# Squares in their own buffer, a fourth PSUM bank in turn, the solve on one engine, one convolution tap and the update keys on ScalarE and GpSimd, and an order table per chunk

## The reference, cut to what matters

```
xn = layernorm(x)
qkv = silu(causal_conv4(xn @ W_qkv.T))            # 2048 channels, 4 taps for each
z = xn @ W_z.T;  beta = sigmoid(xn @ W_b.T);  g = -exp(A_log) * softplus(xn @ W_a.T + dt_bias)
q, k = l2norm per head (8 heads of 64, each used by 2 of the 16 value heads);  v: 16 heads of 64
for t:  S = S * exp(g_t);  d = (v_t - k_t S) * beta_t;  S += k_t (x) d;  o_t = q_t S
x = x + (norm_weight * rmsnorm(o) * silu(z)) @ W_out.T
h = rmsnorm(layernorm(x)) * norm_w;  scores = softmax(h @ router_w.T), 32 experts, the top 4 of each token
x = x + layernorm(x) + sum over 4 of w_e * (silu(h w1_e) * (h u_e)) w2_e + shared expert(h)
```

## Time and profile before

| what | value |
|---|---|
| median of 3 runs | 1326.2 us (1325.64 to 1330.1) |
| profiled execution, its own time | 1323.6 us |
| its span | 1321.7 us |
| busy PE / DVE / POOL / ACT | 989.4 / 823.2 / 618.0 / 455.4 us |
| mean granted clock of TensorE | 0.832 |
| DMA, mean over the span | 125 GB/s |

### The profile page before, as it was taken

One profiled execution on the slowest core, in us unless ns is written; L12 is line 12 of the kernel. 1 busy time (PEld: TensorE's weight loads), 2 busy tenths in 40 slices (PEclk: granted clock), 3 DMA queues, 4 the chain that ended last, 5 costly groups with the idle time before them and its releaser, 6 DMA issues.

```text
span 1321.7 us, 32155 instructions
## 1 busy us (share of the span) xinstructions
PE 989.4 (75%) x12359; PEld 810.8 (61%) x12359; DVE 823.2 (62%) x1947; ACT 455.4 (34%) x890; POOL 618.0 (47%) x907
## 2 busy tenths in 40 slices
PE   0673687787688879868787986878685799998950
PEld 0662675676577667657666765766675457776730
DVE  5169469569848956984895698489544243333335
ACT  1331422542253244225324422532422124444420
POOL 2036248447545744764484476448343013554530
PEclk9776789698778969877896987789588699999985
DMA  5270232505253360535336152533685922444437
GB/s 206 83 190 18 70 85 52 163 22 153 71 152 104 103 173 23 153 66 157 103 98 173 29 153 66 157 97 83 185 282 186 358 69 81 126 134 123 118 124 222
DMA packets 182356, 165.61 MB, mean 125 GB/s; under 512 B 75699, under 2 KB 174908, under 8 KB 181312
## 3 DMA queue, kind: packets, MB, share of 16 engines
q1 hardware_dynamic: 172272, 144.60, 38.9%
q0 software_dynamic: 7632, 16.87, 4.0%
q10 hardware_dynamic: 2304, 2.10, 0.5%
HBM read 66.03 MB, written 101.55 MB: 127 GB/s over the span
## 4 chain that ended last, share of the span: by engine, by line
PE 44%; DVE 34%; issue 9%; DMA 6%; ACT 4%; SPq 1%; POOL 1%; DVEq 0%; POOLq 0%; ACTq 0%
DVE arena L785 9%; PE ps L1039 5%; PE ps L1187 5%; PE ps L1249 5%; DVE arena L427 5%; DVE arena L424 4%; PE ps L1171 3%; PE ps L1102 3%; PE ps L1048 2%; PE ps L1092 2%; PE ps L1111 2%; PE ps L1272 2%; DMA out<-work 2%; PE ps L1156 2%; DMA work<-htd 2%
## 5 line engine op out<-in xcount | busy, mean ns | idle before, releaser
L785 DVE SCALAR_TENSOR_TENSOR arena<-ps,cw,arena 128x256 f32<-128x256 f32 x384 | 156.1, 475 | 84.2 <-ACT arena L600 83.1
L1039 PE MATMUL ps<-work,arena 128*128 128x259 f32 x512 | 162.6, 454 | 26.9 <-DVE arena L785 24.6
L557 POOL DMA_INDIRECT picked<-work x95 | 93.4, 983 | 111.4 <-DVE work L974 66.1
L1039 PEld LDWEIGHTS ps<-work,arena 128*128 128x128 f32 x512 | 107.4, 222 | 55.7 <-DVE arena L785 29.4
L600 ACT ACTIVATE arena<-ps,cw 128x256 f32<-128x256 f32 x128 | 60.2, 470 | 198.9 <-PE ps L1039 198.4
L546 POOL DMA_INDIRECT slotted<-hr,slots x64 | 63.3, 989 | 138.7 <-DVE slots L931 124.0
L964 DVE TENSOR_TENSOR work<-work,ps 128x128 f32<-128x128 f32 (+1 forms) x111 | 34.0, 307 | 140.6 <-ACT work L700 116.1
L477 POOL TENSOR_TENSOR rn<-rin,mhalf 128x16 f32<-128x16 f32 x16 | 46.5, 2906 | 153.7 <-DVE rin L791 153.7
L1249 PE MATMUL ps<-arena,work 128*128 x380 | 100.7, 387 | 7.4 <-issue 6.2
L427 POOL TENSOR_TENSOR arena<-arena 128x60 f32<-128x60 f32 (+29 forms) x248 | 92.1, 372 | 19.4
L424 POOL TENSOR_TENSOR arena<-arena 128x60 f32<-128x60 f32 (+29 forms) x248 | 89.4, 360 | 24.1 <-DVE arena L827 7.8
(11 more groups left out here) (221 smaller groups left out, 2234.7 us busy)
## 6 DMA issues: line engine op xcount, KB each, us to landing
slotted<-blank SPq DMA_DIRECT2D x17, 4128.0 KB
arena<-in_w SPq DMA_DIRECT2D x2, 6528.0 KB, 20.1
work<-slotted SPq DMA_DIRECT2D x95, 129.0 KB
arena<-tab SPq DMA_DIRECT2D x64, 128.0 KB, 3.5
work<-tab SPq DMA_DIRECT2D x64, 128.0 KB
arena<-picked SPq DMA_DIRECT2D x16, 512.0 KB, 4.6
work<-xtd SPq DMA_DIRECT2D x8, 259.0 KB, 3.4
arena<-in_x SPq DMA_DIRECT2D x1, 2048.0 KB, 8.4
```

What stands on the lines that cost most here:

```text
L557: g.indirect_dma_start(out=picked, out_offset=bass.IndirectOffsetOnAxis(ap=to, axis=0), in_=yrow[:, j % SLOTS, :], in_offset=None, bounds_ ...
L785: v.scalar_tensor_tensor(out=acc_, in0=bank_of("proj", p, s_, i)[:, k:k + W2], scalar=cw[:, u, k:k + 1], in1=acc_, op0=ALU.mult, op1=ALU.a ...
L1039: ins = mm(to[:, 0:WX], wqkv[:, k, m:m + P], xt2[:, p % 3, k, :], start=k == 0, stop=k == KD - 1)
```

## The change

It has seven parts.

1. The squares get a buffer of their own, `sq` (`carve(KT, W2)`), four rows instead of eight, so `silu` no longer waits for the solve of the pair before; it waits for `ss_mm` of the two groups before. `at` holds 6 chunks instead of 8.
2. Tap 1 moves from DVE to ACT: `mul` writes taps 0 and 1 into two places, DVE's `tap` does taps 2 and 3 (four instructions), and a new item `sum` on POOL adds the two places before `silu`.
3. The solve's elimination runs on DVE alone, all columns. A new ACT item `lg` (three copies) puts `ntx` in order, so that `lx` is one transpose of 128 partitions.
4. `up` goes. A new POOL item `ktb` multiplies the keys by the negative beta and decay for the chunk, `ku` multiplies them with the copied u (`us`) and waits for `ue` and `ktb`; it has 16 products of 64x64 instead of 8 of 64x128.
5. KU shares the bank of UR, and the bank so freed is the fourth one in turn. `z`, `ht`, `rt` and `rank` take banks in turn too; `yt` and `op` keep W3.
6. `tc` is split in `ta` (the copies that need only the transposes) and `tc`; `ht` on ACT in `hr` and `htb`.
7. The table is new, with `PAIR = 95.20`, a time for each step of the solve, and for each of a pair's four chunks and two blocks a row of its own. It starts a pair's convolution while the pair before is being solved.

The diff, cut to its core:

```diff
-PAIR, CHUNK = 84.0, 21.0
-FRONT = [(20, "blank"), (60, "xload"), (62, "dload"), (10.5, "ss", 0), (16.9, "kt", 0), (17, "kt", 1), (13, "ssq", 0), (13.2, "rpow", 0),
+TURNS = 4
+PAIR = 95.20
+FRONT = [(-89.34, "nd", 0), (-88.1, "nd", 1), (-60.93, "proj", 0, 0), (-59.88, "proj", 0, 1), (-59.83, "xload"), (-59.78, "blank"),
...
-        return [("tap", 6 * (8 * p + ix[0]) + 5 + ix[1])]
+        return [("tap", 4 * (8 * p + ix[0]) + 3 + ix[1])]
+    if name == "z":
+        return [("zs_out", 4 * p + ix[0] + 1)]
...
+        ktb = carve(KR, DH)
+        sq = carve(KT, W2)
-        W = banks[0:3]
-        W3, KS, QS, UR, KU = banks[3:8]
-        O, U = (KS, QS), (UR, KU)
+        W = banks[0:TURNS]
+        W3, KS, QS, UR = banks[TURNS:8]
+        KU = UR
+        O, U = (KS, QS), (UR, W[3])
...
+                if name == "sum":
+                    p, s_ = ix
+                    f = 8 * p + s_
+                    pool.wait_ge(S["tap"], 4 * f + 4)
+                    pool.wait_ge(S["mul_out"], 4 * f + 4)
+                    g.tensor_tensor(ca[:, f % 2, :, :], ca[:, f % 2, :, :], conv_to(p, s_), ALU.add).then_inc(S["sum_out"], 1)
+                if name == "ktb":
+                    n, = ix
+                    pool.wait_ge(S["kn_out"], n // 2 + 1)
+                    wait(pool, S["ku_mm"], n)
+                    g.tensor_tensor(ktb.rearrange("p (kt r) d -> p kt r d", r=2),
+                                    ktok[:, n // 2 % 4, n % 2, :, :].unsqueeze(2).broadcast_to([P, KT, 2, DH]),
+                                    ndb[:, n, :].rearrange("p (kt r) -> p kt r", r=2).unsqueeze(3).broadcast_to([P, KT, 2, DH]),
+                                    ALU.mult).then_inc(S["ktb_out"], 1)
...
+                    u, from_ = TILE_ORDER[2 * s_ + i], bank_of("proj", p, s_, i)
+                    a.activation(ca[:, f % 2, i, :], from_[:, 0:W2], ACT.Copy, scale=cw[:, u, 0:1]).then_inc(S["mul_out"], 1)
+                    a.activation(conv_to(p, s_)[:, i, :], from_[:, 1:1 + W2], ACT.Copy, scale=cw[:, u, 1:2]).then_inc(S["mul_out"], 1)
                 if name == "silu":
-                    act.wait_ge(S["tap"], 6 * f + 6)
+                    act.wait_ge(S["sum_out"], f + 1)
                     a.activation(dst, ca[:, f % 2, :, :], ACT.Silu).then_inc(S["silu_out"], 1)
-                        wait(act, S["pm_mm"], p)
-                        wait(act, S["lx_out"], 4 * p)
+                        wait(act, S["ss_mm"], 2 * p + s_ // 2)
+                if name == "lg":
+                    p, = ix
+                    act.wait_ge(S["at_out"], 4 * p + 4)
+                    wait(act, S["pm_mm"], p)
+                    a.activation(xr, ntx[:, 0:H, :], ACT.Copy).then_inc(S["lg_out"], 1)
+                    act.wait_ge(S["lg_out"], 3 * p + 1)
+                    for e in range(2):
+                        own = slice(C * e + H, C * e + C)
+                        a.activation(xr[own], ntx[own, H:C, :], ACT.Copy).then_inc(S["lg_out"], 1)
...
-                    for k in range(1, TAPS):
+                    for k in range(2, TAPS):
                 if name == "lx":
-                    for q in range(4):
-                        v.transpose(nl[rows], ntx[rows, own, :]).then_inc(S["lx_out"], 1)
+                    v.transpose(nl, xr).then_inc(S["lx_out"], 1)
-                if name == "up":
-                    v.tensor_tensor(rr, by_head(UR), ndb[:, n, :].unsqueeze(2).broadcast_to([P, KR, DH]), ALU.mult).then_inc(S["up_out"], 1)
...
                 if name == "ku":
-                    pe.wait_ge(S["up_out"], n + 1)
+                    pe.wait_ge(S["ue_out"], n + 1)
+                    pe.wait_ge(S["ktb_out"], n + 1)
-                    for kt in range(KT):
+                    for h in range(KR):
                         for hp in range(2):
+                            ins = mm(KU[half(hp), DH * h:DH * h + DH], ktb[half(hp), h, :], us[half(hp), h, :], start=True, stop=True)
```

197 lines of the change are left out of this document (100 added, 97 removed), and 20 rows, old and new, of tables (CHAIN, FRONT, TAIL).

## The result

The changed kernel takes 1274.0 us (median of 4 runs, 1271.0 to 1275.3) against 1328.2 us for the kernel before on the same chip: a ratio of 0.959, 95% interval 0.956 to 0.962. It was timed again beside the kernel before in two later sessions: 0.958 (0.955 to 0.961) and 0.960 (0.957 to 0.964). So it is faster by 4.1%, 54 us. The forecast was 1219 us, 107 us faster. The time lies in the wide range, but not in 1190 to 1250, and half of the gain did not come.

What follows compares the result with a forecast made beforehand. No engine is full; DVE and PE alternate, waiting for each other. Span 62 + 82 + 695 (seven periods) + 69 + 306.7 = 1214.7 us, so 1219 us; range 1190 to 1250, for 8 in 10 1168 to 1290.

Steps and rivals of the forecast that it cites:

- `sum` as covered in a pair: Between taps and `silu`: 9.6 us a pair if on the path, covered by the solve's steps, thinly in the first pair.
- Holds in the solve: DVE's solve beside twelve large POOL instructions, each holding it 0.75 us for 60% of the time: 5.4 us.
- The solve at 29: DVE's solve of 62 instructions a pair: 29 us taken, between bounds of 22.8 and 40.5 us.
- The rival that the port decides: Powers and twelve large POOL instructions hold DVE's solve, 40.5 us instead of 29: period 110, 1275 us; chance 0.17.
- Holds elsewhere: DVE's work outside the solve: it reads PSUM and isn't held, so no cost.
- The periods: Seven stretches from `pm` to `pm`: 102 us each, less 19 for the first and last, 695 us.
- The first stretch: From the first projection to the first `pm`: 82 us, from 76.5, with 4 for sums in the bare path.
- half B: From `lx` to the next `pm`, where DVE has the work: 50.6 us.
- half A: From `pm` to `lx`, where PE has the work: 51.1 us, including 2 us of waits.
- the last stretch with the end: From the last `pm` to the span's end: 69 us to the last chunk's output, then an unchanged 306.7.
- the wait of 6.4 us for the power: DVE's wait for a power on POOL, before `yn`: it would be gone.
- the fourth bank: Its gain counted as already in the halves' sum; a missing bank would cost PE some 2 us more in each half.

Runs made afterwards that it cites:

- e15_small_pool: Changed kernel with `sum` over 8 of 256 columns and `kqs`, `ktb`, `sd` mostly over 2 of 64 columns of a head: 1170.8 us, ratio 0.901.
- e7_sumsmall: Changed kernel with the `sum` on POOL over 8 of 256 columns only, every wait kept: 1230.0 us, ratio 0.928.
- e14_sum_aside: Changed kernel with `sum` at full size on GpSimd but into a buffer nobody reads, `silu` waiting for the taps alone: 1249.3 us, ratio 0.960.
- e10_first: Changed kernel with, in pair 0 alone, `kk`, `nt` and the solve ahead and the value groups among the solve: 1281.0 us, ratio 0.984.
- e9_su: Changed kernel with the state updates of the third and fourth chunk earlier in the table: 1259.4 us, ratio 0.968.
- e12_banks3: Changed kernel with three banks in turn instead of four, key updates in a bank of their own: 1315.0 us, ratio 1.011.
- e4_blanks: Changed kernel with the fill of blank rows (`blanks`) issued after `tm`: 1269.6 us, ratio 0.973.

## Why the forecast was right in kind and wrong in size

The step that failed is the price of `sum` and of GpSimd's holds. The forecast counted `sum` as covered in a pair, and priced the holds as "12 x 0.75 x 0.6 = 5.4 us", in the solve alone. What the runs showed is 13.2 us of holds a pair (`e15_small_pool`) and a `sum` that costs 40 us of the time (`e7_sumsmall`), about half of it by its own duration between the taps and `silu` (`e14_sum_aside`). Point by point:

- **Holds in the solve:** 5.4 forecast, 6.3 measured (`e15_small_pool`). The solve at 29 was right (27.7 and gaps). The rival that the port decides had its time, 1275 us, nearly right, but by powers that hold the solve. That was luck: they don't; the large instructions do, and beside more than the solve.
- **Holds elsewhere:** forecast nothing ("the rest reads PSUM and isn't held"), measured 6.9 us a pair: the scan, the `yn` products, the norms and some of the router's small steps read SBUF alone. Two inputs are not needed: the router's cast L966, with one, has a mean of 0.54 us instead of 0.17, and at 409.35 us it takes 0.85 beside a `ktb`. A row of the kernel before, shown below, could have said so: the norm of a block with 869 ns, against 479 in `e15_small_pool`; the earlier trace rows showed a hold in the solve and I looked for it nowhere else. Not all of it is new, since `kqs` and `sd` stood beside VectorE in the kernel before too. New is `sum`: 0.61 us by eight, 4.9 us a pair (`e7_sumsmall`).

```profile
L898 DVE SCALAR_TENSOR_TENSOR hr<-row,small,fw 128x256 f32<-128x256 f32 x16 | 13.9, 869 | 3.6 <-POOL small L477 3.6
```

- **The periods, +35:** with a small `sum` seven periods take 699.9 us, the forecast 695. So holds and duration of `sum` are 30 of the 35 us.
- **The first stretch, +22:** `sum` is 9 to 11 of it (155.2 in `e7_sumsmall`, against 164.3 in the same session and 166.0 in the first trace). A group there is a bare chain of taps, `sum`, `silu` and the next first tap, about 5 us each (the taps start at 95.03, 100.79, 106.42 and 110.98 us), not 1.6 and a share of 4. For the rest the likeliest cause is that this pair's value groups all stand ahead of `lx`, where I priced only the groups of the next pair. No run shows it as such: `e10_first` moves them behind and the first `pm` comes 12 us earlier, but all of that and more comes back in the first period.
- **The late state updates:** 1 to 2 us of a period (`e9_su`), for which half B had no term. TensorE's waits in half A stayed small, 2.9 us, as said.
- **Right:** half A (48.3 for 51.1), `lx` at 1.25 us, `lg` at 1.06 + 2.13 = 3.2 us, the last stretch with the end (377.1 for 375.7), the wait of 6.4 us for the power gone from before `yn` (1.2 us left), and `tm` still with stops (5.9 us instead of 7.7).
- **Taken for granted:** the fourth bank. The halves were summed as if no bank were missing. That was right, but it was the hinge: without the fourth the time is 1315 us, a period 6.1 us longer where the forecast had 4 for a missing bank (`e12_banks3`).

Open is how `sum`'s cost splits between hold and duration beyond "about half", and what the changed kernel takes in a session without stops in `tm`: it was never timed in one. `e4_blanks` with 1269.6 us suggests that its stops are mostly hidden, so that its gain would be nearer 3% there.

## What to carry to other kernels

Before moving work to GpSimd, add to its own time what it takes from VectorE: here each instruction of 128x512 with SBUF operands cost VectorE 0.55 to 0.66 us on the mean of all, so an engine that was half idle was no free place. Price such a move against every instruction of VectorE that may lie beside it, the tiny ones included (here all but those that read PSUM), and look for the price by shrinking the suspect, not by deleting it. Where a sum assumes that buffers are never short, test that assumption by a run of its own: here it was worth more than any cost that the sum had missed in a period.

## What was not expected of the hardware

- The same program differs by session: 1297.6 to 1305.5 us in three and 1324.9 to 1328.4 in the other three. The traces put it into `tm` (30.8 us of records and 0.2 of stops against 39.9 and 17.9). What sets it is open: one chip number has 1305.5 us in one session and 1328.4 in another. A change must be compared within one session.
- A VectorE product of 128x16 elements takes 0.97 us on the mean where `sum` and the other large GpSimd instructions are about and 0.19 where they are small.
- GpSimd is held too: beside two scans on VectorE, from 97.09 us in the changed kernel, a `sum` takes 2.11 us, against 1.27 for one at 102.86, beside VectorE instructions that read PSUM.
- A power of 2.92 us on GpSimd with 16 elements a partition does not hold VectorE: the solve instructions of 252 elements beside it keep 0.41 and 0.42 us.
- At 447 us TensorE comes back from an idle 4.97 us at the 1.2 GHz level (granted clock 0.50), and `ss` and `kt` after it cost 7.2 us; another `ss`, at 439.23, takes 2.03 us instead of 3.58.
